# A gated delta-rule kernel: the output products on four quarters of the TensorE array, and the update of S from a copy that GpSimd scaled

## The reference, cut to what matters

```
kS = k_t . S                                   # S is 64 x 128
S  = a_t * (S - b_t * outer(k_t, kS)) + outer(k_t, v_t)
o_t = q_t . S
```

## Time and profile before

| what | value |
|---|---|
| median of the runs | 4844.67 us |
| the profiled execution, its own time | 4845.65 us |
| its span, first to last instruction | 4843.8 us |
| mean granted TensorE clock | 0.970 |
| PE / PEld / DVE / ACT / POOL busy | 85% / 60% / 74% / 58% / 27% |

### The profile page before, as it was taken

How to read it: one execution, slowest core, us unless ns; L and a number is a source line. 1 busy time by engine, 2 the same in 40 slices (tenths; PEclk the granted TensorE clock), 3 DMA queues, 4 the chain that set the end, 5 groups by cost and what they waited for, 6 DMA issues and landing times. The chain is left out here.

```text
span 4843.8 us, 155608 instructions
## 1 busy us (share of the span) xinstructions
PE 4096.6 (85%) x59788; PEld 2913.1 (60%) x59788; DVE 3575.8 (74%) x8216; ACT 2828.8 (58%) x4519; POOL 1312.3 (27%) x1318
## 2 busy tenths in 40 slices
PE   5888888888888888888888888888888888888855
PEld 4666665666666665666666666666656666665644
DVE  5777777777777777777777777777777777777745
ACT  2566656565565656556565655666565556656534
POOL 2222222222222222222222222222222222222211
PEclk9999999999999999999999999999999999999977
DMA  1211111111111111121111111111111111111111
GB/s 52 43 37 41 39 37 41 38 42 38 42 37 38 41 37 42 38 42 37 39 40 36 41 38 42 37 40 39 37 41 38 42 38 41 38 37 41 37 39 40
DMA packets 877985, 191.77 MB, mean 40 GB/s; under 512 B 816000, under 2 KB 873600, under 8 KB 877952
## 3 DMA queue, kind: packets, MB, share of 16 engines
q1 hardware_dynamic: 871648, 173.49, 17.1%
q0 software_dynamic: 6304, 17.84, 1.3%
HBM read 136.16 MB, written 55.06 MB: 39 GB/s over the span
## 5 line engine op out<-in xcount | busy, mean ns | idle before, releaser
L826 DVE SCALAR_TENSOR_TENSOR cv<-ps,w_v,cv 128x512 f32<-128x512 f32 x768 | 576.7, 751 | 553.3 <-ACT cv L691 535.1
L826 DVE SCALAR_TENSOR_TENSOR cv<-ps,w_kq,cv 128x512 f32<-128x512 f32 x768 | 574.4, 748 | 87.5 <-ACT cv L691 69.3
L607 PE MATMUL ps<-QG,S 64*128 64x64 f32 x4096 | 431.7, 274 | 3.3
L610 PE MATMUL ps<-PT,U 64*128 64x64 f32 x4096 | 429.2, 272 | 0.0
L458 PE MATMUL ps<-Lm,k_all 128*128 128x512 f32 x768 | 419.3, 627 | 0.0
L691 ACT ACTIVATE cv<-ps,w_kq 128x512 f32<-128x512 f32 x256 | 175.9, 687 | 399.2 <-PE ps L447 399.2
L1002 POOL TENSOR_TENSOR qn<-sl,sq 128x512 f32<-128x512 f32 x128 | 161.8, 1264 | 906.2 <-ACT sq L729 906.2
L467 PE MATMUL ps<-sq,k_all 128*128 128x512 f32 x512 | 287.6, 644 | 125.9 <-ACT ex L698 125.8
L706 ACT ACTIVATE sl<-cv 128x512 f32<-128x512 f32 x256 | 161.3, 630 | 395.1 <-DVE cv L826 395.1
L447 PE MATMUL ps<-xnT,w_v 128*128 (+1 forms) x1024 | 296.2, 410 | 97.0 <-DVE Nd L841 53.0
L607 PEld LDWEIGHTS ps<-QG,S 64*128 64x128 f32 x4096 | 342.5, 188 | 30.5 <-issue 30.5
(11 more groups left out here) (183 smaller groups left out, 10441.2 us busy)
## 6 DMA issues: line engine op xcount, KB each, us to landing
scrN<-Nd SPq DMA_DIRECT2D x256, 128.0 KB, 2.4
Z<-scrZ SPq DMA_DIRECT2D x256, 128.0 KB, 2.9
X<-scrX SPq DMA_DIRECT2D x512, 64.0 KB, 2.6
w_v<-wtab SPq DMA_DIRECT2D x128, 132.0 KB, 2.2
w_kq<-wtab POOLq DMA_DIRECT2D x128, 132.0 KB, 2.4
wo_s<-wo SPq DMA_DIRECT2D x128, 128.0 KB, 2.4
NS<-scrN SPq DMA_DIRECT2D x128, 64.0 KB, 2.6
scrZ<-XT SPq DMA_DIRECT2D x128, 64.0 KB, 2.5
```

The source lines that it names most:

```text
L607: nc.tensor.matmul(o_cols(h, b), unit(S, b)[a:z], sub_block(BD["QG"], 0, b, a, z), start=True, stop=False)
L610: last = nc.tensor.matmul(o_cols(h, b), unit(U, b)[a:z], sub_block(BD["PT"], 0, b, a, z), start=False, stop=True)
L826: nc.vector.scalar_tensor_tensor(cv4[:, j], pj[:, :, k:k + C], tap(j, k), cv4[:, j], ALU.mult, ALU.add).then_inc(conv.sem, 1)
```

## The change: what it does

The output products are split by halves of the value columns: each of the two heads' products (rows 0 to 63, rows 64 to 127 of the array) becomes two with 64 output partitions, so that four 64x64 quarters of the array are used, and pe_o issues twice as many matmuls. GpSimd computes Sg = gamma*S in two instructions of 128x512, after the decay products of its body and ahead of qn. dve_s waits for Sg too, and adds the four units of dS from PSUM and the half of Sg with one instruction of 128x512. Sg is a new tile.

```diff
@@ -110,6 +110,7 @@
         Rr = sb("Rr", NB * P)
         U = sb("U", NB * P)
         S = sb("S", NB * P)
+        Sg = sb("Sg", NB * P)
         oo = sb("oo", 1024)
         Nd = sb("Nd", 512)
         NS = sb("NS", 272)
@@ -388,6 +389,7 @@
         o_mm = sig("o_mm", 2)
         ds_mm = sig("ds_mm", 2)
         s_ok = sig("s_ok", 2)
+        sg_ok = sig("sg_ok", 2)
         o_sq = sig("o_sq", 2)
         ms_mm = sig("ms_mm", 2)
         ms_ln = sig("ms_ln", 2)
@@ -592,9 +594,9 @@
                                                 start=True, stop=True)
                 last.then_inc(u_mm.sem, 1)
 
-        def o_cols(h, b):
-
-            return ps[:, (4 + h) * 512 + b * C:(4 + h) * 512 + (b + 1) * C]
+        def o_cols(h, b, d):
+
+            return ps[d:d + 64, (4 + h) * 512 + b * C:(4 + h) * 512 + (b + 1) * C]
 
         def pe_o(pe, m):
             pe.wait_ge(qg_ok.sem, qg_ok.at(m))
@@ -604,11 +606,13 @@
                 pe.sem_inc(pe_go.sem, 1)
                 for b in GROUPS[g]:
                     for h, (a, z) in enumerate(HALF):
-                        nc.tensor.matmul(o_cols(h, b), unit(S, b)[a:z], sub_block(BD["QG"], 0, b, a, z),
-                                         start=True, stop=False)
+                        for d in (0, 64):
+                            nc.tensor.matmul(o_cols(h, b, d), S[a:z, b * P + d:b * P + d + 64], sub_block(BD["QG"], 0, b, a, z),
+                                             start=True, stop=False)
                     for h, (a, z) in enumerate(HALF):
-                        last = nc.tensor.matmul(o_cols(h, b), unit(U, b)[a:z], sub_block(BD["PT"], 0, b, a, z),
-                                                start=False, stop=True)
+                        for d in (0, 64):
+                            last = nc.tensor.matmul(o_cols(h, b, d), U[a:z, b * P + d:b * P + d + 64], sub_block(BD["PT"], 0, b, a, z),
+                                                    start=False, stop=True)
             last.then_inc(o_mm.sem, 2)
 
         def pe_ds(pe, m):
@@ -924,9 +928,8 @@
         def dve_s(dve, m, g):
             dve.wait_ge(o_mm.sem, o_mm.at(m))
             dve.wait_ge(ds_mm.sem, ds_mm.at(m, g + 1))
-            for b in GROUPS[g]:
-                last = nc.vector.scalar_tensor_tensor(unit(S, b), unit(S, b), stR[:, 8 + b:9 + b], slot(6 + g, b), ALU.mult, ALU.add)
-            last.then_inc(s_ok.sem, 1)
+            dve.wait_ge(sg_ok.sem, sg_ok.at(m, g + 1))
+            nc.vector.tensor_tensor(half(S, g), bank(6 + g), half(Sg, g), ALU.add).then_inc(s_ok.sem, 1)
 
         def dve_on(dve, m, groups=(0, 1)):
             for g in groups:
@@ -996,6 +999,8 @@
             nc.gpsimd.tensor_tensor(v3(ex, 0), v3(ex, 0), bcast(stP[:, 8:16], C), ALU.mult).then_inc(dmul.sem, 1)
             pool.wait_ge(dec_ex.sem, dec_ex.at(n, 2))
             nc.gpsimd.tensor_tensor(v3(ex, 1), v3(ex, 1), over(kc(K_MLE, C), NB, C), ALU.mult).then_inc(dmul.sem, 1)
+            if m is not None:
+                pool_decay_s(pool, m)
             pool.wait_ge(nrm_rn.sem, nrm_rn.at(n, 2))
             if not first(n):
                 pool.wait_ge(gram_p.sem, gram_p.at(n - 1))
@@ -1011,10 +1016,21 @@
                 pool.wait_ge(o_mm.sem, o_mm.at(m))
             nc.gpsimd.tensor_tensor(half(BD["QG"], 0), qn[:], half(ex, 2), ALU.mult).then_inc(qg_ok.sem, 1)
 
+        def pool_decay_s(pool, m):
+            pool.wait_ge(stR_ok.sem, stR_ok.at(m))
+            for g in range(2):
+                if not first(m):
+                    pool.wait_ge(s_ok.sem, s_ok.at(m - 1, g + 1))
+                gam = stR[:, 8 + 4 * g:12 + 4 * g].rearrange("p (b o) -> p b o", o=1).to_broadcast([P, 4, P])
+                nc.gpsimd.tensor_tensor(half(Sg, g).rearrange("p (b v) -> p b v", b=4), half(S, g).rearrange("p (b v) -> p b v", b=4),
+                                        gam, ALU.mult).then_inc(sg_ok.sem, 1)
+
         def pool_body(pool, m, n):
             if n is not None:
                 pool_weights(pool, n)
                 pool_prepare(pool, m, n)
+            else:
+                pool_decay_s(pool, m)
 
 
 
```

## The result

The changed kernel takes 4766.28 us (median of 4 runs, 4764.98 to 4768.39), against 4845.01 before (the median of four runs with one more than above): a ratio of 0.9837, 95% interval 0.9824 to 0.9849. The forecast was 4762. The profiled execution's span is 4766.6 us (77 less than before), its mean granted clock 0.932 instead of 0.970.

The account below looks back on a forecast made before the run. Bound by a loop of VectorE's queue, then ScalarE, convolution, KB, Gram, Nd and memory. Terms -0.86 + 0.25, with 0.04 more for queue place, gave -0.65 us a step, x 127 = -83: 4762 us, range 4715 to 4900.

Parts of the forecast that it names:

- S update: VectorE's S halves: one wide instruction at 0.68 us replaces 1.11, twice a step, saving 0.86 us a step.
- Output products: TensorE's output stage: 128 matmuls 15 ns apart take 1.9 us, ending some 1.7 earlier, gaining nothing on the loop.
- QG: GpSimd's QG follows NM at once and delays VectorE's 64x18 product, costing 0.25 us a step; bounds 0 and 0.33.
- The clock: TensorE's longer pause brings more clock falls at less each, keeping the present cost of 0.37 us a step.
- Rival 1: GpSimd's queued scalings begin before the held KB, which waits for one (4900 us) or both (5032); chance 0.20.
- Rival 2: TensorE's clock falls in every step at the full price of 1.17 us: 4865 us; chance 0.14.
- Rival 3: Output quarters sharing rows do not overlap: in pairs 4736 us, chance 0.07; fully one by one 5150, chance 0.02.
- Rival 4: Something else on the loop is late next, so the 0.86 us is not gained: 4845 us; chance 0.07.

Follow-up runs that it names:

- before_fill: The kernel before the change with one idle 128x512 TensorE product, read by nobody, in the pause ahead of the transposed keys: 4801.82 us.
- s_only_fill: The kernel before with the S update of the change alone, output products left as 64x128, plus one idle product behind the transposed keys: 4726.40 us.
- q_only_fill: The kernel before with the output products on four quarters alone, plus three idle products in the pause ahead of the transposed keys: 4814.38 us.
- kb_fill: The full change with two idle products ahead of the transposed keys, and GpSimd's second decay product and both scalings of S moved behind KB: 4645.83 us.
- s_only: The kernel before with the S update of the change alone, output products left as 64x128, no idle products: 4745.32 us, ratio 0.9795.
- late_fill: The run late with one idle 128x512 product behind the Gram matrix of queries and one behind the transposed keys: 4495.26 us, ratio 0.9278.
- late: The full change with GpSimd's NM and QG moved behind the substitution's 14th instruction: three executions of 4697.77 to 4699.30 us, one of 4532.03.

## Why the prediction was right, and where only its sum was

The loop was read rightly: VectorE's queue from XT to the second convolution, then ScalarE, KB, Gram, Nd and memory. Every gain or loss above is one of that loop's segments.

**S update**: forecast -0.86 a step and 0.04 more for its place in the queue, -0.90; measured -0.89 (7.94 to 7.05, before_fill to s_only_fill).

**Output products**: forecast 1.9 us at 15 ns each, measured 1.88. The floor of about 25 ns that the Trainium skill gives (TensorE: Matmul & The Clock Gate, section Back-to-back issue gap) would have made 3.2, an estimate from that page. The trace does not agree: its 128 instructions start 15 ns apart on the mean.

**QG**: forecast +0.25, measured +0.09 alone (q_only_fill) and +0.13 with the S update. In the step shown the 64x18 product ends 2.73 us after XT's start, before 2.54: 0.19, but 0.07 of it is XT, which met NM earlier (1.11 against 1.04). Over 115 steps the 64x18 product ends 2.67 us after XT's start, before 2.53: 0.14. The forecast had QG's end right (it moves forward by 0.24, from 2.50 to 2.26 after XT's start), but let the held 64x8 product start there. The trace has it end there (2505.13, with QG's end at 2505.11), and the 64x18 product ends 0.40 us behind QG, not 0.5. This term was too large by more than 0.1.

**The clock**: "I take the present 0.37, more falls at less each." More falls at less each was right (125 of them for 75 us, 0.6 us each, against 41 for 43, 1.05 each), the total was not: 75 / 127 = 0.59 a step, 0.22 more than forecast, and 0.25 more than the kernel before really paid (43 / 127 = 0.34). This is the largest error. The short steps of 34.2 us without a fall, which the forecast expected to see, did not come: each step has one.

**stR**: not in the sum. When the first tap is late or the convolution moves, the copy stR runs clear of GpSimd's Lm, and the stretch from conv 0 to conv 2 is 10.84 instead of 11.29. In the change this gives back 0.11 even without falls.

So the forecast of -0.65 a step against the measured -0.59 hides three errors: 0.25 for the clock one way, 0.12 for QG and 0.11 for stR the other. That they cancel, and that 4762 lies 4 us from 4766, is luck. With the clock held up the forecast would have been -0.65 and the truth is -0.87 (111 us in all).

**Rival 1** (GpSimd keeps the inputs) fell: KB goes ahead of the queued scalings, and the first of them waits for KB. Likewise XT ends at 2503.91, 0.02 after NM, though QG is recorded from 2503.86. That the held KB is what lengthens the first scaling, the run kb_fill shows: 1482 ns beside it, 1041 behind it. The Trainium skill (SBUF — State Buffer, section Who interferes with whom) says that issue order decides who blocks, and these rows agree; its sentence on a whole instruction held, which the prediction used, is written there for VectorE's two-port mode, while of a product with both inputs in SBUF, such as KB, it says that it contends with GpSimd's reads. **Rival 2** (every step at full price) was right in the number of falls and wrong in their price (0.6 us each, not 1.17). **Rival 3** fell with the 1.88 us.

**Rival 4** was dismissed with "nothing else of the loop hangs on another engine within 0.6 us". That sentence was wrong: ScalarE's SiLU of v was within 0.1 us of ending last in the kernel before (2519.73 against 2519.79), and once VectorE's queue is shorter it does (s_only's wait of 1.49 us), and only the quarters, which move the norm ahead of it 1.8 us earlier, kept it off the loop. The claim that the quarters "on the loop gain nothing" is right for the kernel before (q_only_fill: 13 us slower) and wrong beside the S update, where they bring 36 us (4726.4 to 4690.8), and in late_fill, where they bring 231. These figures are with the clock held up. As the clock falls, the quarters make the change 21 us slower than the S update alone (4766.3 against 4745.3).

## What to carry to other kernels

Price a part in the company of the other parts: time it with the others present and without, since the same edit, with the clock held up, lost 13 us, gained 36 and gained 231. When an engine off the path gets faster, look at what its clock does in the longer pause; an idle product in that pause is a cheap test of the cost, and may stay as the cure. A tiny instruction that takes a microsecond is worth a look at what GpSimd does beside it: here moving two GpSimd instructions, with the pause filled, gave 196 us beside the quarters, and nothing without them.

## What the runs showed of the hardware that was not expected

The clock's falls and the steps can lock: in the run late both come every 34.13 us, and the executions split into 4698 and 4532 us. And a VectorE instruction that waits for GpSimd's reads gets in between two queued GpSimd instructions, though the record of the second starts before it: the first scaling is recorded from 2529.72 and its pair takes 2.48 us, 0.4 more than twice L999's 1.04, as KB reads until 2530.31. Behind KB (kb_fill) a scaling takes 1.04.
